# Attention units in the order tile 0, 3, 0, 3, ... then 1, 2, 1, 2, ..., and value products in two steps of ten

## The reference

```python
q = rmsnorm(x @ w_qa, q_norm_w) @ w_qb        # 16 heads, 128 + 64 (rotary)
kv = rmsnorm(kv_c, kv_norm_w) @ w_kvb         # kv_c: 64 latents, k_rope: 64 shared
...
scores = jnp.einsum('blhd,bmhd->bhlm', q, k) * scale
scores = jnp.where(mask[None, None], scores, -1e30)     # causal
attn = jax.nn.softmax(scores, axis=-1)
out = jnp.einsum('bhlm,bmhd->blhd', attn, v)
return out.reshape(B, L, H * DV) @ w_o
```

## Time and profile before

| | us |
|---|---|
| median of 3 runs (1338.85 to 1340.66) | 1339.31 |
| the profiled execution | 1338.7 |
| its span | 1336.9 |
| TensorE busy | 1231.2 (92%) |
| VectorE busy | 813.2 (61%) |
| ScalarE busy | 454.2 (34%) |

### The profile page before, as it was taken

One profiled execution on the slowest core, in us unless ns is written; L12 is line 12 of the kernel. 1 busy time (PEld: TensorE's weight loads), 2 busy tenths in 40 slices (PEclk: granted clock), 3 DMA queues, 4 the chain that ended last, 5 costly groups with the idle time before them and its releaser, 6 DMA issues.

```text
span 1336.9 us, 19470 instructions
## 1 busy us (share of the span) xinstructions
PE 1231.2 (92%) x6004; PEld 760.4 (57%) x6004; DVE 813.2 (61%) x2238; ACT 454.2 (34%) x1041; POOL 378.8 (28%) x464
## 2 busy tenths in 40 slices
PE   6999999999999899998989999997578899899988
PEld 3566566555655556556556777775235446465454
DVE  6367767787578966785533333334576776676431
ACT  2455525453445425452201111110232533424311
POOL 1243013362425412362250000115364271510200
PEclk9799999999999999999999999998679899999999
DMA  9999999999900100011348888983111011100000
GB/s 317 413 420 420 420 421 419 420 419 417 420 35 28 68 1 1 1 52 44 101 129 256 259 266 273 285 260 118 48 55 48 24 52 36 37 12 17 0 16 16
DMA packets 89422, 235.48 MB, mean 176 GB/s; under 512 B 12769, under 2 KB 23681, under 8 KB 89089
## 3 DMA queue, kind: packets, MB, share of 16 engines
q1 hardware_dynamic: 70912, 192.54, 38.9%
q0 software_dynamic: 9216, 25.18, 5.9%
q10 hardware_dynamic: 9216, 16.78, 3.3%
HBM read 66.70 MB, written 167.77 MB: 175 GB/s over the span
## 4 chain that ended last, share of the span: by engine, by line
PE 69%; DVE 23%; issue 4%; POOL 2%; ACT 1%; DMA 1%; SPq 1%; ACTq 0%; POOLq 0%; DVEq 0%
PE bank L1329 5%; PE bank L529 5%; PE bank L617 4%; PE bank L488 4%; PE bank L1309 4%; PE bank L489 4%; PE bank L555 4%; DVE negmax L861 4%; PE bank L1582 3%; DVE r L872 3%; PE bank L1571 3%; PE bank L1565 3%; PE bank L538 3%; PE bank L1335 3%; PE bank L1294 2%
## 5 line engine op out<-in xcount | busy, mean ns | idle before, releaser
L708 ACT ACTIVATE r<-bank,negmax 128x128 f32<-128x128 f32 (+3 forms) x256 | 135.2, 528 | 174.3 <-DVE negmax L861 173.8
L529 PE MATMUL bank<-r 128*128 128x512 f32 (+3 forms) x512 | 184.3, 443 | 0.0
L861 DVE TENSOR_REDUCE negmax<-bank 128x1 f32<-128x128 f32 (+3 forms) x256 | 124.5, 487 | 44.6 <-PE bank L530 41.6
L972 POOL TENSOR_TENSOR r<-r,tables 128x256 f32<-128x256 f32 x56 | 42.0, 749 | 330.5 <-ACT r L689 330.3
L538 PE MATMUL bank<-tables,r 128*128 128x128 f32 x640 | 115.0, 278 | 12.2 <-DVE r L872 11.6
L1196 POOL DMA_INDIRECT sent<-r,slots x96 | 93.9, 978 | 99.8 <-DVE slots L1117 40.1
L1411 DVE COPY r<-bank 128x512 f32<-128x512 f32 x64 | 41.2, 686 | 120.5 <-PE bank L1335 76.2
L538 PEld LDWEIGHTS bank<-tables,r 128*128 128x128 f32 x640 | 72.7, 141 | 65.9 <-DVE r L872 31.4
L872 DVE TENSOR_SCALAR r<-r,rrow 128x128 f32<-128x128 f32 (+3 forms) x256 | 104.5, 408 | 0.3
L529 PEld LDWEIGHTS bank<-r 128*128 128x128 f32 x512 | 77.8, 191 | 23.6 <-issue 18.3
L1210 POOL DMA_INDIRECT r<-sent,slots x20 | 21.7, 1085 | 219.1 <-DVEq L1409 212.8
(11 more groups left out here) (266 smaller groups left out, 2390.5 us busy)
## 6 DMA issues: line engine op xcount, KB each, us to landing
sent<-gath SPq DMA_DIRECT2D x8, 16384.0 KB, 94.3
r<-waT_dram SPq DMA_DIRECT2D x64, 304.0 KB, 3.4
r<-sent SPq DMA_DIRECT2D x64, 256.0 KB, 3.4
sent<-r ACTq DMA_DIRECT2D x64, 256.0 KB, 4.1
w2buf<-wcT_dram SPq DMA_DIRECT2D x64, 48.0 KB, 3.5
r<-w_o_dram SPq DMA_DIRECT2D x1, 2048.0 KB, 11.0
sent<-gath SPq DMA_DIRECT2D x2, 1024.0 KB, 57.0
out_dram<-x SPq DMA_DIRECT2D x4, 512.0 KB, 2.9
```

Of the source, the lines that this page charges most:

```text
L529: nc.tensor.matmul(at[:, 0:n], QT[g % 2][:, h, i * P:(i + 1) * P], KT[:, 0:n], start=True, stop=False)
L708: nc.scalar.activation(prob[:, u % 4, 0:(i + 1) * P], bank[SCORE[u % 4]][:, 0:(i + 1) * P], ACT.Exp, bias=negmax[:, u:u + 1], scale=1.0, a ...
L861: nc.vector.tensor_reduce(negmax[:, u:u + 1], bank[SCORE[u % 4]][:, 0:(i + 1) * P], axis=AX.X, op=ALU.max, negate=True).then_inc(A["max"], 1)
```

## The change

A unit is now found by `unit(u)`: in the first eight slots tile 0 and tile 3 by turns, in the last eight tile 1 and tile 2 by turns, the head rising every second slot. Every pair of slots has five key blocks. The value steps are `((0, 3), (1, 2))`, ten products each, on slots 12 and 20, so the step on slot 16 (slot 0 of the next group) is gone; the waits for steps count two for a group. The query products and turns keep their slots and follow the order of tiles 0, 3, 1, 2. Each step copies two tiles on ScalarE. The longest diff parts:

```diff
-        VALUES_AT = {12: 0, 16: 1, 20: 2}
-        VALUE_TILES = ((0, 1), (2,), (3,))
+        VALUES_AT = {12: 0, 20: 1}
+        VALUE_TILES = ((0, 3), (1, 2))
+        ORDER = (0, 3, 1, 2)
+
+        def unit(u):
+
+            return VALUE_TILES[u // (2 * HG)][u % 2], u // 2 % HG
...
             def scores(g, u):
-                i, h = u // HG, u % HG
+                i, h = unit(u)
                 n = (i + 1) * P
                 need(pe, A["exp"], NU * g + u - 3)
                 if h == 0:
-                    pe.wait_ge(A["qte"], TB * g + i + 1)
+                    pe.wait_ge(A["qte"], TB * g + ORDER.index(i) + 1)
...
             def values(g, n):
                 tiles = VALUE_TILES[n]
-                pe.wait_ge(A["pte"], NU * g + HG * (tiles[-1] + 1))
-                need(pe, A["ote"], 3 * g + n)
+                pe.wait_ge(A["pte"], NU * g + 2 * HG * (n + 1))
+                need(pe, A["ote"], 2 * g + n)
...
-                for i in tiles:
-                    c = 2 * P * (i - tiles[0])
+                for m, i in enumerate(tiles):
+                    c = 2 * P * m
...
             def evacuate(g, u):
-                i, h = u // HG, u % HG
+                i, h = unit(u)
                 dve.wait_ge(A["pt"], NU * g + u + 1)
                 if h == 0:
-                    need(dve, A["pv"], 3 * (g - 1) + max(1, i))
+                    need(dve, A["pv"], 2 * (g - 1) + u // (2 * HG) + 1)
```

More of the change, by code:

```diff
@@ L485, in q_product @@
                 hg = g % GROUPS
+                tile = slice(ORDER[i] * P, (ORDER[i] + 1) * P)
                 w1 = wqe1[:, hg * HG:(hg + 1) * HG, :].rearrange("p h c -> p (h c)")
                 w2 = wqe2[:, hg * HG:(hg + 1) * HG, :].rearrange("p h c -> p (h c)")
-                nc.tensor.matmul(bank[at][:], cq1[:, i * P:(i + 1) * P], w1, start=True, stop=False)
-                nc.tensor.matmul(bank[at][:], cq2[:, i * P:(i + 1) * P], w2, start=False, stop=True)\
+                nc.tensor.matmul(bank[at][:], cq1[:, tile], w1, start=True, stop=False)
+                nc.tensor.matmul(bank[at][:], cq2[:, tile], w2, start=False, stop=True)\
                     .then_inc(A["q"], 1)
@@ L533, in transposes @@
             def transposes(g, u):
-                i = u // HG
+                i, _ = unit(u)
                 pe.wait_ge(A["norm"], NU * g + u + 1)
@@ L612, in output @@
                 if i == 0:
-                    pe.wait_ge(A["ote"], 3 * GROUPS * (b + 1))
+                    pe.wait_ge(A["ote"], 2 * GROUPS * (b + 1))
                 if i >= 2:
@@ L692, in qt_copy @@
                 act.wait_ge(A["qt"], TB * g + i + 1)
-                nc.scalar.copy(QT[g % 2][:, :, i * P:(i + 1) * P],
+                nc.scalar.copy(QT[g % 2][:, :, ORDER[i] * P:(ORDER[i] + 1) * P],
                                bank[at][:].rearrange("p (h c) -> p h c", h=HG)).then_inc(A["qte"], 1)
@@ L968, in rope @@
             half = DR // 2
-            c = cosq[:, i, :].unsqueeze(1).to_broadcast([P, HG, DR])
-            s1 = sinq[:, i, 0:half].unsqueeze(1).to_broadcast([P, HG, half])
-            s2 = sinq[:, i, half:DR].unsqueeze(1).to_broadcast([P, HG, half])
+            tile = ORDER[i]
+            c = cosq[:, tile, :].unsqueeze(1).to_broadcast([P, HG, DR])
+            s1 = sinq[:, tile, 0:half].unsqueeze(1).to_broadcast([P, HG, half])
+            s2 = sinq[:, tile, half:DR].unsqueeze(1).to_broadcast([P, HG, half])
             api.tensor_tensor(ta, q[:, :, KVL:QE], c, ALU.mult).then_inc(parts_done, 1)
```

4 lines of the change are left out of this document (2 added, 2 removed).

## The result

| | before | after |
|---|---|---|
| median | 1339.92 us (1338.85 to 1340.66) | 1350.36 us (1348.09 to 1353.14) |
| the profiled execution | 1338.7 | 1348.09 |
| its span | 1336.9 | 1346.2 |

The ratio is 1.0079, 95% interval 1.0059 to 1.0100: slower, by 10 us. The forecast was 1342.0 with a range up to 1347. Direction and place were right; the size was not.

A forecast was written before the change was run, and what follows sets the result against it. TensorE was taken to bound groups with query products, VectorE with ScalarE the four last ones. Terms -5.8 - 2.6 + 0.6 + 0.3 + 3.0 + 7.1 + 0.1 = +2.7 on 1339.3 gave 1342.0 us, range 1334.0 to 1347.0.

The forecast's parts named there:

- The value steps: All 16 groups: three value steps become two of ten products, saving 0.36 us a group, -5.8 us in all.
- The waits in slots 1 and 3 of a row's first group: Query product's waits at each row start: longer scores ahead cover them, -0.66 us a row, -2.6 us for four rows.
- The turn in slot 11: Row 0's first three groups: the turn waits about 0.2 us in each for ScalarE's copy, +0.6 us.
- the product in slot 1: Next group's first query product, rows 1 to 3: waits 0.8 us for the last turn's copy, twice a row.
- A: Rival: the last group isn't slower by waits, slot 0's wait doesn't appear, value steps alone decide; 1333.5 us, chance 0.2.
- B: Rival: slower through the uncovered chain at the next group's first product, +4.6 us, 1346.6 us; chance 0.18.
- against TensorE's own stream that is 4.9 of waits for 1.9: Row 0's last group: TensorE's waits up to the next projection grow from 1.9 to 4.9 us, +3.0 us.
- The last group, row 0: VectorE bounds it and idles in slots 5 and 13; projection 24.75 us after slot 0 for 24.2, +3.0 us.
- The last group, rows 1 to 3: Last group of each later row: TensorE waits 7.6 us for 5.25, +2.35 a row, +7.1 us in all.
- Routing pads the same idle places: Last groups of rows 1 to 3: routing work fills VectorE's idle places; projection at 27.45 us for 27.55.
- The ends of groups in row 0: Next group's first product after the last turn: the max, exp, copy chain of 2.1 us fits, so no wait.
- The last row and its end: Last row: the last-group term of +2.35 us, plus 0.1 us because the output waits for two copies.

The follow-up runs named there:

- set 1: Runs on one chip; meant here: changed kernel with idle matmuls at row ends, 1344.78 us (1.0038), beside the changed kernel again, 1353.08 us (1.0096).
- set 2: Runs on a second chip; meant here: changed kernel with the last groups' `weigh` calls moved from slots 10, 12, 14 to 4, 4, 12: 1377.26 us, 1.0036.
- the steps alone: Kernel before, old order of units kept, with two value steps (tiles 0 and 1, tiles 2 and 3): 1393.09 us, 1.0143.
- the order alone: Kernel before with the new order of units but three value steps (tile 0, tile 3, tiles 1 and 2): 1385.52 us, 1.0080.

## Why the prediction was right or wrong

**What held.** The reading that TensorE bounds the groups with products and VectorE (with the chain behind it) the last ones decides the sign, and the two runs with one order in the last group and the other elsewhere show it. The schedule by hand holds in the places that follow. The value steps: TensorE's excess over its streaming time at the borders of value steps is 1.36 smaller in row 0, for 4 x 0.36 = 1.44. The waits in slots 1 and 3 of a row's first group are gone. The turn in slot 11 waits 0.185 in each of three groups, for 0.2. VectorE idles in slots 5 and 13 of row 0's last group:

```profile
147.80 0.69 DVE L867 TENSOR_REDUCE negmax<-bank 128x1 f32<-128x512 f32 x1 [1.56 <-PE bank L536]
...
159.23 0.56 DVE L867 TENSOR_REDUCE negmax<-bank 128x1 f32<-128x384 f32 x1 [1.54 <-PE bank L536]
```

for "about 1.6" and "about 1.5", beside 1.55 and 0.50 in the earlier trace rows. The new wait of the reciprocal for the exponential is there too (0.20 twice). And the product in slot 1 waits for the turn's copy as foreseen:

```profile
230.49 1.13 PE L494 MATMUL bank<-r 128*128 128x512 f32 x2 [0.51 <-ACT r L699]
```

**Rivals.** A (the cover holds) fell: no part of it appears. The Trainium skill's rule behind it (Perfetto Trace Analysis, Optimization Strategy: interleaving regimes may help) did not help here: the waits for probabilities went from 11.6 to 20.0 us. The prediction's reason, that the lag of three slots bridges the two regimes already, fits this and was not tested by itself. B's mechanism is there, but at 0.43 us in each of its six places, where the forecast had 0.8 and B more. Two slips in the recorded numbers: A's 1333.5 lies outside the range that was to hold it (from 1334.0), and half of 0.45 with B's 0.18 is 0.405, where 0.43 was given for slower.

**The step that failed: "against TensorE's own stream that is 4.9 of waits for 1.9".** The sum took those waits at their length. In rows 1 to 3 they stand close together at the row end, and behind them the granted clock is 0.5: the projection of the next row is 1.40 longer at the ends of rows 1 and 2, the last value step 2.2, and the transposes ahead some 0.3 each time. These 5.9 us (5.2 net between the traces of set 1, 8.3 between its medians) are more than half of the 10.5 and in no term. All stretches that the forecast rested on showed 1.00, and it took the clock for a constant of attention. The Trainium skill (TensorE: Matmul & The Clock Gate, "A second HAM failure mode: psum-queue depth-cycling") tells of a bf16 kernel in which frequent short idle times between groups of matmuls make the clock swing between its two rates. The trace agrees: 0.5 and 1.0 are the only values, and the longest wait ahead of a fall is 1.52 us; here the products are f32.

**Terms that were too small.**
- *The last group, row 0*: +3.0 forecast. TensorE's wait for probabilities over the whole row grew by 3.6 (summed from start-to-start distances). The projection starts 25.3 us after slot 0's scores, for 24.75 forecast and 24.2 before. The row end was put at too little; three waits stand there, with the clock still at 1.00:

```profile
161.68 0.55 PE L544 MATMUL bank<-tables,r 128*128 128x128 f32 x3 [0.51 <-DVE r L878]
162.80 0.44 PE L544 MATMUL bank<-tables,r 128*128 128x128 f32 x2 [0.57 <-DVE r L878]
163.83 0.55 PE L544 MATMUL bank<-tables,r 128*128 128x128 f32 x3 [0.60 <-DVE r L878]
```


- *The last group, rows 1 to 3*: +2.35 each. With the clock's 1.7 taken off, rows 1 and 2 are some 0.7 longer than before, where the terms gave -1.44 - 0.66 + 0.1 + 2.35 = +0.35. The calls of `weigh` are 0.94 us each (314.02 - 313.08), and the one of slot 14 stands between two units of VectorE's queue, which makes the wait of 1.52 for the second (with the calls elsewhere it is 0.2 to 0.6, set 2):

```profile
312.75 0.41 DVE L878 TENSOR_SCALAR r<-r,rrow 128x384 f32<-128x384 f32 x1
313.08 0.28 DVE L1140 SCALAR_TENSOR_TENSOR scratch<-r,scratch 128x64 f32<-128x64 f32 x1
...
314.02 0.56 DVE L867 TENSOR_REDUCE negmax<-bank 128x1 f32<-128x384 f32 x1
...
314.88 0.34 DVE L878 TENSOR_SCALAR r<-r,rrow 128x256 f32<-128x256 f32 x1
```

 "Routing pads the same idle places" was wrong: slot 5, where VectorE idles, has no call.
- *The ends of groups in row 0*: put at nothing ("in row 0 that fits"); two borders wait 0.155 each.
- *The last row and its end*: +0.35 and +0.1 forecast, +3.30 measured, some 2.5 of it the clock and 0.8 waits.

Without the clock the sum of all terms measures 4.6 us in the trace of the change, and 5.5 with the idle products and their own cost, for +2.7 forecast. That alone would have been 1344 to 1345, inside the range; the clock took it out.

**Still open.** On three of four chips TensorE waits longer at the end of the last groups of rows 1 to 3 than on the first, in single waits of up to 2.8 us; with the old order and three steps it also waits in slot 7, mostly 1.6 to 2.1 us, where the others have 0.6 at most. In many of these places TensorE, VectorE and ScalarE are idle together, for up to 1.1 us. The profile names no releaser that was late: VectorE starts 3.48 after its last work (above) on scores that TensorE had finished 1.9 us earlier. Loading of instructions doesn't explain it as far as the trace shows: a packet of an instruction queue starts at 296.4 in slot 7, but at 296.2 in the first chip's trace too, and none starts between 306 and 321. It isn't there in row 0, nor on the first chip, and no run tried to remove it. It is the smaller part of what these chips add: of 42 us in the kernel before, 27.5 lie behind attention, which nothing here looks into. Nor is it shown how many us the place of the `weigh` calls gives by itself: no run differs from the changed kernel in it alone on the same chip.

## What to carry to other kernels

Before changing an order, ask for each boundary what the engine downstream does with several small waits in a row, and price the work behind them at half clock as well: the three waits at a row's end cost another 1.7 to 2.5 us behind them. A saving on the bounding engine counts only in the stretches where it is the bound; order and step sizes are to be tried apart and together, since here they don't add: in row 0 the steps alone cost 2.7 us, the order alone 1.6, both 2.4. And run the kernel before, with a profile, on the chip of every comparison, and look at the whole spread: the profiled execution can be the fastest of one kernel and among the slowest of another.

## What the runs showed of the hardware

- The granted clock fell to 0.5 behind waits of 0.75, 1.52 and 0.59 us with two or three transposes between them, at the ends of rows 1 to 3. Behind waits of 0.51, 0.57 and 0.60 in row 0 it stayed at 1.00, and so it did in the kernel before on that chip behind 0.64, 0.86, 0.52 and 0.57, with a value step after the second.
- On the first chip idle products that nobody reads, 11 in a row end, kept it at 1.00 through attention. On the others every kernel with idle products at the row ends still had one to four falls. They cost 0.2 us in row 0 where they lay in waits, 1.1 us where they didn't.
- The kernel before took 1339 us on one chip and 1373 to 1379 on three others; row 0 with its last group in the old order and no idle products took 140.2 on all four. In attention the difference is 4.3 to 5.2 us in each later row, in longer waits at slot 7 and the row end and the clock behind them; behind attention it is 27.5 us more, unexplained.
- The 0.36 us that a value step has beside its products, whatever its size, shows in the result: 1.36 us less at the borders of value steps for four steps fewer.
